# Two-layer gated cross-attention with routed experts on one core: layer 0 written as one block; in layer 1 the last head group ahead of the end of the ranking, its transfers on two queues, the biases loaded last

## The chip, the core and the metric

The program runs on one core of a Trainium2 chip. A core has five engines that run their own instruction streams and meet only at semaphores: TensorE (PE, matrix products into the PSUM banks; PEld are its weight loads), VectorE (DVE), ScalarE (ACT), GpSimd (POOL) and SyncE (SP, which mostly issues transfers). Transfers run on 16 DMA engines that all queues share. The metric is the device time of one execution in microseconds, lower is better.

## What is computed

A sequence `x` of 2048 rows of 256 values passes through two layers. Each layer adds gated cross-attention to a context of 1601 rows of 192 values (16 heads of 16), then a gated expert network:

```python
x = x + tanh(g_xattn[0]) * cross_attention_0(layernorm(x), ctx)      # softmax over 1601 keys, then Wo
x = x + tanh(g_ffn[0])   * (shared_swiglu(h) + top1_expert_swiglu(h * sigmoid(max_logit)))   # h = layernorm(x)
x = x + tanh(g_xattn[1]) * mlp(cross_attention_1(layernorm(x), ctx)) # relu(o @ W1 + b1) @ W2 + b2
h = layernorm(x)
y = mixed_top2_experts(h) + h          # relu(h @ W1[e] + b1[e]) @ W2[e] + b2[e], weighted by a softmax of two logits
x = x + tanh(g_ffn[1]) * (gamma * layernorm(y) + beta)
```

There are 8 experts in each layer.

## The kernel before

The 2048 rows stand on 128 partitions, 16 tiles of 128 rows. Every engine has its own program, written out in the order in which it runs; a wait on a semaphore holds up all that is behind it on that engine. A *block* is a piece of program for all five engines: at its end the engines meet in a barrier before the next one starts.

Layer 0 is made of three blocks. The first is the **preparation** (`prepare(0)`): it loads `x`, the context and weights, normalizes, projects keys, queries and values, writes bf16 parts of them to DRAM, and ends with `unsafe`, a flag that says whether the scores could overflow. The second block opens with `asked`: each engine loads `unsafe` into a register and branches, and normally jumps over a part that finds the largest scores. Then comes **attention**: four query blocks of 512, four groups of four heads each, 13 chunks of 128 keys in each (52 steps `w` for each query block). `scores` (L1539) makes the scores, ACT the exponentials (L1868), `weigh` (L1564) the weighted values. For each group DVE copies the result, spreads the sum of the exponentials, takes the reciprocal and multiplies (`group_copy`, `group_norm`, and `last_group` for the very last group, which does it in two halves), and SP moves four heads of it to where the projection reads them (L2487, and `gather_last`, L2497, with eight transfers for the halves). After attention come the shared experts, the routing, and the keys of layer 1. The third block is the **expert loop**: POOL fetches the rows of a tile by index (`fetch_rows`, L1145), PE turns them (`turn_rows`, L1242), DVE or ACT copies them, `up` (L1255) and `down` (L1269) are the two products, and POOL stores the result by index (L1456). This block goes on with the preparation of layer 1 and ends in a barrier that also clears the semaphores.

Layer 1 is one more block. Its last part matters here. Twelve of its sixteen row tiles are ranked early: in step `COUNTS_AT` = 44 of the last query block `counts_first` counts them on PE, then `rank_first` on DVE works out each token's slot, builds one-hot rows (`in_row`, L2282, for 24 slots in one instruction) and the expert of each tile; `lists_first` on PE (L1710) turns them into lists, and `places` on DVE into row numbers, on which POOL's fetches and ACT's copies of expert weights wait. Behind `rank_first` DVE adds the bias of the projection to `x` and runs `own_tail`: `last_group`, `places`, then the work on the projection. PE runs `lists_first`, then `keep_warm` (products of the identity with itself into a bank nobody reads, L466), then `last_projection` (L1786, L1795), whose halves wait for the two halves of the last head group, then the expert loop. In this loop ACT works on the 17 early tiles (`first_scalar`) and POOL adds the bias `eb2`; DVE meanwhile ranks the rest. SP loads the down weights of the 8 experts (L1199, 512 KB each) and their biases spread over the partitions (L1195, 128 KB each) in turn, then `gamma` and `beta`. `down(0)` waits for all sixteen loads:

```python
if i == 0:
    pe.wait_ge(s_e, 16 * (2 if l else 3) * E)
```

## Time and profile before

| | us |
|---|---|
| median of 3 runs | 1403.71 |
| lowest, highest run | 1403.46, 1404.62 |
| the profiled execution | 1401.74 |
| its span, first to last instruction | 1400.0 |
| mean granted PE clock in it | 0.985 of full |
| PE, ACT, DVE, POOL busy | 1324.1, 987.5, 721.0, 193.8 |

Times in rows are counted from the start of the span. The profiled execution is 1.74 us longer than its span and 1.97 us shorter than the median of the runs. The clock of PE is either full (2.4 GHz) or half of it (1.2 GHz), so a value between means a stretch with both. A row of the timeline gives start, duration, engine, line, operation and shapes, and in brackets how long the engine had been idle and what it had waited for. Products of f32 values take two passes and so count as two instructions: the 12 of `keep_warm` show as x24.

### The profile page before, as it was taken

How to read it: one execution, taken by the hardware profiler on the slowest of the kernel's cores; microseconds unless marked ns; L12 is line 12 of the kernel's file. 1: busy time of each engine (PE TensorE's matmuls, PEld its weight loads, DVE VectorE, ACT ScalarE, POOL GpSimd, SP SyncE). 2: the span in 40 equal slices, each digit the busy share in tenths (PEclk: the TensorE clock that was granted, in tenths of full speed). 3: DMA queues.
4: the chain of work that ended last, by engine and by line, in shares of the span. 5: the costliest groups of instructions: out<-in, count | busy, mean ns of one | idle time of the engine just before them, and what ended most of it. 6: DMA issues, size and time to landing. Idle time of an engine off the chain costs nothing. (4 is left out here: it accounts for less than half of the span.)

```text
span 1400.0 us, 33588 instructions
## 1 busy us (share of the span) xinstructions
PE 1324.1 (95%) x13844; PEld 729.6 (52%) x13844; DVE 721.0 (52%) x1415; ACT 987.5 (71%) x1263; POOL 193.8 (14%) x211
## 2 busy tenths in 40 slices
PE   7899999999999999899988999999999997999994
PEld 4433343343433555899964333433433533889983
DVE  7466634544352435433356474585485487442436
ACT  4699999999999334223256998798799695376532
POOL 2000000000000232133220000000000000287740
PEclk9999999999999999999998999999999999999998
DMA  7771010010110642411147500020010130522214
GB/s 204 184 131 29 21 28 18 21 30 21 30 27 20 228 156 71 136 50 50 35 123 187 104 21 18 17 59 21 17 59 21 51 111 25 191 65 70 76 60 175
DMA packets 66966, 103.53 MB, mean 74 GB/s; under 512 B 10524, under 2 KB 48674, under 8 KB 65916
## 3 DMA queue, kind: packets, MB, share of 16 engines
q1 hardware_dynamic: 60860, 85.10, 22.2%
q0 software_dynamic: 5952, 16.26, 3.7%
q8 instruction: 111, 1.82, 0.6%
q14 instruction: 43, 0.35, 0.1%
HBM read 69.04 MB, written 27.79 MB: 69 GB/s over the span
## 5 line engine op out<-in xcount | busy, mean ns | idle before, releaser
L1868 ACT ACTIVATE arena<-ps 128x1024 f32<-128x1024 f32 x528 | 521.1, 1151 | 47.1 <-PE ps L1539 46.1
L1539 PE MATMUL ps<-arena 99*32 99x512 bf16 x6528 | 454.0, 385 | 11.3 <-issue 7.6
L1539 PEld LDWEIGHTS ps<-arena 99*32 99x32 bf16 x6528 | 167.6, 96 | 372.1 <-issue 163.0
L1564 PE MATMUL ps<-arena 128*32 128x512 f32 x2176 | 333.8, 596 | 0.6 <-ACT xn L1861 0.4
L1868 ACT ACTIVATE wqkv<-ps 128x1024 f32<-128x1024 f32 x260 | 269.3, 1144 | 21.2 <-PE ps L1539 21.1
L1564 PE MATMUL ps<-wqkv,arena 128*32 128x512 f32 x1056 | 186.4, 593 | 0.1
L1255 PE MATMUL ps<-work,arena 128*128 128x128 f32 x1184 | 144.5, 277 | 2.0 <-DVE work L1344 1.0
L1255 PEld LDWEIGHTS ps<-work,arena 128*128 128x128 f32 x1184 | 142.9, 194 | 5.7 <-DVE work L1344 1.5
L1269 PE MATMUL ps<-arena,work 128*128 x496 | 117.6, 380 | 2.0 <-DMA arena<-in_eb 1.6
L1564 PEld LDWEIGHTS ps<-arena 128*32 128x32 f32 x2176 | 79.7, 111 | 58.2 <-issue 4.7
L2019 DVE RECIPROCAL work<-work 128x512 f32<-128x512 f32 x30 | 100.6, 3353 | 1.0
L1269 PEld LDWEIGHTS ps<-arena,work 128*128 128x128 f32 x496 | 89.4, 190 | 12.7 <-issue 3.0
L1145 POOL DMA_INDIRECT work<-xn_early,fetch x17 | 21.1, 1243 | 491.8 <-DVE fetch L2372 474.6
L2592 POOL TENSOR_TENSOR arena<-arena 128x512 f32<-128x512 f32 x12 | 17.5, 1458 | 477.7 <-ACT arena L1888 477.7
L1316 ACT ACTIVATE work<-ps 128x512 f32<-128x512 f32 x23 | 13.8, 598 | 98.0 <-PE ps L1255 98.0
L1154 ACT ACTIVATE arena<-arena 128x1024 f32 x62 | 65.5, 1059 | 18.8 <-DVE fetch L2372 12.1
L1456 POOL DMA_INDIRECT y_tok<-work,dest x62 | 62.1, 1002 | 117.0 <-DVE work L1370 83.5
L1344 DVE COPY work<-ps 128x256 f32<-128x256 f32 x45 | 19.1, 424 | 97.7 <-PE ps L1242 82.7
L2010 DVE SCALAR_TENSOR_TENSOR work<-xn,last_v,ps 128x512 f32<-128x512 f32 x30 | 22.4, 745 | 81.6 <-PE ps L1564 81.3
L2105 DVE TENSOR_TENSOR work<-ps,b 128x512 f32<-128x512 f32 x14 | 9.7, 691 | 94.0 <-PE ps L1597 94.0
L1564 PEld LDWEIGHTS ps<-wqkv,arena 128*32 128x32 f32 x1056 | 43.7, 111 | 25.5 <-issue 0.6
L1973 DVE TENSOR_SCALAR xn<-ps 128x1024 f32<-128x1024 f32 x12 | 14.7, 1224 | 78.5 <-PE ps L1539 78.5
(327 smaller groups left out, 1477.7 us busy)
## 6 DMA issues: line engine op xcount, KB each, us to landing
arena<-in_ew SPq DMA_DIRECT2D x16, 512.0 KB, 4.7
arena<-q_img SPq DMA_DIRECT2D x32, 192.0 KB
arena<-y_tok SPq DMA_DIRECT2D x12, 512.0 KB, 7.0
arena<-k_img SPq DMA_DIRECT2D x8, 624.0 KB, 12.9
q_img<-work SPq DMA_DIRECT2D x18, 256.0 KB, 2.8
k_img<-work SPq DMA_DIRECT2D x21, 208.0 KB, 2.5
arena<-q_img SPq DMA_DIRECT2D x32, 128.0 KB
arena<-in_rg SPq DMA_DIRECT2D x8, 512.0 KB, 7.1
```

Source lines behind the costliest of these rows:

```text
L1145: nc.gpsimd.indirect_dma_start(out=rows_in[i % ROWBUFS], out_offset=None, in_=xn_early if i < L.first else xn_img[l], in_offset=bass.Indir ...
L1154: nc.scalar.activation(w_now[i % 2][0].rearrange("p k n -> p (k n)"), w_gate[l][:, bass.ds(e, 1), :, :].rearrange("p a k n -> p (a k n)"), ...
L1255: last = nc.tensor.matmul(ps[:, 2 + 2 * (i % 2) + n, f * P:(f + 1) * P], w_now[i % 2][n][:, k, f * P:(f + 1) * P], rowsT[i % 2][:, k, :], ...
L1269: last = nc.tensor.matmul(ps[:, 6 + i % 2, 0:D], hT[i % 2][:, k, :], w_down[:, bass.ds(e, 1), k, :].rearrange("p a n -> p (a n)"), start=( ...
L1344: nc.vector.tensor_copy(rowsT[i % 2], ps[:, i % 2, 0:D].rearrange("p (k n) -> p k n", n=P)).then_inc(s_tc, 1)
L1456: nc.gpsimd.indirect_dma_start(out=y_tok[l], out_offset=bass.IndirectOffsetOnAxis(ap=dest[:, i:i + 1], axis=0), in_=rows_out[i % 2], in_of ...
L1539: last = nc.tensor.matmul(ps[i * VW:(i + 1) * VW, buf + j, :], keys, q2[0:ROWS + SHIFT, h, :], start=True, stop=True, skip_group_check=True)
L1564: last = nc.tensor.matmul(ps[j * VW:(j + 1) * VW, 6 + g % 2, :], v_aug[:, c, HG * g + j, :], exps, start=(c == 0), stop=(c == NC - 1), ski ...
L1868: nc.scalar.activation(probs[n % RING], ps[:, buf:buf + 2, :], ACT.Exp, scale=SCALE).then_inc(s_exp, 1)
L2010: nc.vector.scalar_tensor_tensor(out=pv_sb, in0=last_exp[:, g % 2, :], scalar=last_v[:, g:g + 1], in1=ps[:, 6 + g % 2, :], op0=ALU.mult, o ...
L2019: nc.vector.reciprocal(sums, sums).then_inc(s_inv, 1)
L2592: nc.gpsimd.tensor_tensor(sh_hT[:, f, :], sh_hT[:, f, :], sh_act[:, n % 2, :], ALU.mult).then_inc(s_hm, 1)
```

## The change

**Layer 0 in one block.** The three blocks become one. Each engine runs its preparation, its attention part and its expert loop without a barrier between them. What the barriers ensured is now waited for: `asked` waits for a semaphore on `unsafe`, PE for the copied values and POOL's padding of them ahead of its part, SP for the sums of key norms ahead of `loop_sync`.

**Layer 1.** `COUNTS_AT` goes from 44 to 42. `rank_first` stops after half of the one-hot rows; then comes `last_group`, then the second half, the expert numbers and the rest as before. `keep_warm` is called with 24 ahead of `lists_first` and with 4 behind it, instead of with 12 behind it. `gather_last` runs on SP for heads 0 and 1 and on ACT, ahead of `first_scalar`, for heads 2 and 3. SP loads the eight down weights first and then the eight biases, which count on `s_ln` now; `down(0)` waits for the weights alone, POOL and DVE for `s_ln`.

In `group_norm` and `last_group` two semaphores of their own become the chain that the rest of DVE's program uses, with the same waits.

```diff
-COUNTS_AT = 44
+COUNTS_AT = 42
@@ pad_v
-                chain(nc.gpsimd.memset(v_aug[other, NC - 1, i::2, 0:DH], 0.0))
+                last = nc.gpsimd.memset(v_aug[other, NC - 1, i::2, 0:DH], 0.0)
+            last.then_inc(s_vpad, 1)
@@ prepare, tensor
-                if l == 1:
+                if l == 0:
+                    pe.wait_ge(s_va, NC)
+                    pe.wait_ge(s_vpad, 1)
+                else:
                     keep_warm(3, 8)
@@ prepare, vector
-                chain(nc.vector.tensor_scalar(unsafe[0:1, :], tops[0:1, 2:3], SAFE * SAFE / SCALE ** 2, None, ALU.is_gt))
+                nc.vector.tensor_scalar(unsafe[0:1, :], tops[0:1, 2:3], SAFE * SAFE / SCALE ** 2, None, ALU.is_gt).then_inc(s_un, 1)
@@ layer
-            if l == 0:
-                with nc.Block() as block:
...
-                    block.gpsimd(prep_pool)
...
             def asked(eng):
+                eng.wait_ge(s_un, l + 1)
                 return eng.If(eng.value_load(unsafe[0:1, 0:1], min_val=0, max_val=1) > 0)
@@ load_biases
-                eng.dma_start(eb2[:, e, :], spread(a["eb2"][e], D)).then_inc(s_e, 16)
+                eng.dma_start(eb2[:, e, :], spread(a["eb2"][e], D)).then_inc(s_ln, 16)
...
+            def gather_last(eng, heads):
+                g = NG - 1
+                for i in range(2):
+                    cols = slice(i * 2 * P, (i + 1) * 2 * P)
+                    eng.wait_ge(s_on, NB * NG + i)
+                    for j in heads:
+                        h = HG * g + j
+                        eng.dma_start(oT[(h % 8) * DH:(h % 8 + 1) * DH, h // 8, cols],
+                                      o_norm[j * VW:j * VW + DH, g % 2, cols]
+                                      ).then_inc(s_oh2 if i else s_oc[g % 2], 16)
@@ loop_tensor, down
-                        pe.wait_ge(s_e, 16 * (2 if l else 3) * E)
+                        pe.wait_ge(s_e, 16 * (1 if l else 3) * E)
@@ loop_vector, and loop_pool likewise
-                    dve.wait_ge(s_ln, 32)
-                    dve.wait_ge(s_e, 16 * 2 * E)
+                    dve.wait_ge(s_ln, 16 * (2 + E))
@@
             def first_scalar(act, between):
+                gather_last(act, range(HG - 2, HG))
                 act.wait_ge(s_pl, 1)
@@ tensor
+                    if l == 0:
+                        prep_tensor(pe)
                     max_tensor(pe)
@@ lists_first
-                        pe.wait_ge(s_row, 1)
                         for i in range(of.slots):
+                            if i % (of.slots // 2) == 0:
+                                pe.wait_ge(s_row, i // (of.slots // 2) + 1)
@@
                     if l == 1:
+                        keep_warm(0, 24)
                         lists_first()
-                        keep_warm(0, 12)
+                        keep_warm(0, 4)
                         last_projection()
...
                         k_norm(3)
+                        loop_tensor(pe)
@@ vector, own_tail
-                        last_group()
                         places(first_lists, 6, 0)
@@ rank_first
-                        lists_of(of, end, L.pieces()[0], 0, 1)
+                        lists_of(of, L.pieces()[0])
+                        rows_of_lists(of, 0, 2)
+                        return end
@@
-                        rank_first()
+                        end = rank_first()
+                        last_group()
+                        rows_of_lists(first_lists, 1, 2)
+                        experts_of_lists(first_lists, end, 0)
@@ sync
-                    gather_last()
+                    gather_last(sp, range(HG - 2 * l))
                     sp.wait_ge(s_pv, NB * NG * NC)
...
                             load_down(sp, e)
+                        for e in range(E):
                             load_biases(sp, e)
...
-                    if l == 1:
-                        loop_sync(sp)
+                    if l == 0:
+                        sp.wait_ge(s_kn, 4)
+                    loop_sync(sp)
@@ end of layer
-            if l == 0:
-                with nc.Block() as block:
-                    block.sync(loop_sync)
...
-                    block.gpsimd(loop_pool)
```

The instructions of PE between the end of attention in layer 1 and the expert loop, before (L1564 are the last weighings, L1710 the lists, L466 the warming products, L1786 and L1795 the projection):

```order
L1564 MATMUL ps<-wqkv,arena 32x512 x2
L1564 MATMUL ps<-arena 32x512 x10
L1710 MATMUL ps<-ctxT 128x36 x24
L466 MATMUL ps<-ident 128x128 x12
L1786 MATMUL ps<-work,w 128x256 x16
L1795 MATMUL ps<-w,work 128x256 x16
```

and after:

```order
L1568 MATMUL ps<-wqkv,arena 32x512 x2
L1568 MATMUL ps<-arena 32x512 x10
L466 MATMUL ps<-ident 128x128 x24
L1717 MATMUL ps<-ctxT 128x36 x24
L466 MATMUL ps<-ident 128x128 x4
L1793 MATMUL ps<-work,w 128x256 x16
L1802 MATMUL ps<-w,work 128x256 x16
```

Twice as many warming products stand ahead of the lists, and the lists' second half has a wait of its own inside its row.

DVE in the same place, before (L2282 the one-hot rows, L2042 to L2054 the last head group, L2360 the first operation of the places):

```order
L2282 TENSOR_TENSOR ctxT<-iota_row,rankf 128x3072
L2287 TENSOR_TENSOR ctxT<-iota_tile,ends 128x119
L2290 TENSOR_REDUCE tilef<-ctxT 128x17
L2291 CAST tile_e<-tilef 128x17
L2406 SCALAR_TENSOR_TENSOR x<-b,tgate,x 128x512 x2
L2042 SCALAR_TENSOR_TENSOR work<-xn,last_v,ps 128x512
L2046 STREAM_SHUFFLE work<-work 128x512
L2050 RECIPROCAL work<-work 128x256
L2054 TENSOR_TENSOR work<-work 128x256
L2050 RECIPROCAL work<-work 128x256
L2054 TENSOR_TENSOR work<-work 128x256
L2360 COPY pad<-ps 128x17
```

and after:

```order
L2290 TENSOR_TENSOR ctxT<-iota_row,rankf 128x1536
L2052 SCALAR_TENSOR_TENSOR work<-xn,last_v,ps 128x512
L2056 STREAM_SHUFFLE work<-work 128x512
L2059 RECIPROCAL work<-work 128x256
L2062 TENSOR_TENSOR work<-work 128x256
L2059 RECIPROCAL work<-work 128x256
L2062 TENSOR_TENSOR work<-work 128x256
L2290 TENSOR_TENSOR ctxT<-iota_row,rankf 128x1536
L2297 TENSOR_TENSOR ctxT<-iota_tile,ends 128x119
L2300 TENSOR_REDUCE tilef<-ctxT 128x17
L2301 CAST tile_e<-tilef 128x17
L2426 SCALAR_TENSOR_TENSOR x<-b,tgate,x 128x512 x2
```

The head group stands ahead of the second half of the one-hot rows, of the expert numbers and of the bias, with the places behind all of them.

## Rows read from the trace of the kernel before

**Rows 1.** Part 1 of the page: busy time, share, instructions.

```profile
PE 1324.1 (95%) x13844; PEld 729.6 (52%) x13844; DVE 721.0 (52%) x1415; ACT 987.5 (71%) x1263; POOL 193.8 (14%) x211
```

**Rows 2.** Timeline, preparation to attention in layer 0: start, us, engine, line, operation.

```profile
59.74 0.60 PE L906 MATMUL ps<-ident,top 128*1 128x128 f32 x4
...
61.00 0.14 DVE L979 TENSOR_SCALAR unsafe<-tops 1x1 int32<-1x1 f32 x1
61.19 0.27 SPq L525 DMA_DIRECT2D last_value<-work  x1
63.30 6.91 PE L1539 MATMUL ps<-arena 99*32 99x512 bf16 x60 [2.96 <-issue]
```

**Rows 3.** Timeline, shared experts to expert loop in layer 0.

```profile
567.40 0.51 PE L472 MATMUL ps<-head_rows,w 128*104 128x16 bf16 x8
...
567.63 2.02 SPq L1199 DMA_DIRECT2D arena<-in_rd  x4
...
568.98 0.42 DVE L2472 TENSOR_REDUCE norms<-ps 104x4 f32<-104x256 f32 x1
...
570.31 0.41 PE L1242 MATMUL ps<-ident,work 128*128 128x128 f32 x2 [2.40 <-PEq L1510]
...
570.76 0.42 DVE L1344 COPY work<-ps 128x256 f32<-128x256 f32 x1 [1.37 <-PE ps L1242]
...
571.24 5.47 PE L1255 MATMUL ps<-work,arena 128*128 128x128 f32 x32 [0.52 <-DVE work L1344]
```

**Rows 4.** Stretches: us, busy (count) per engine, then PE clock, DMA share, GB/s.

```profile
63.30:73.25 9.95, 9.91 (x84) 3.02 (x88) 5.23 (x9) 6.77 (x8) 0.00 (x0) 0.50 0.85 170
571.60:575.10 3.50, 3.50 (x20) 3.50 (x19) 0.86 (x1) 0.00 (x0) 0.34 (x1) 0.51 1.04 340
745.80:749.20 3.40, 1.81 (x16) 1.34 (x14) 2.54 (x7) 0.00 (x0) 0.00 (x0) 1.00 0.83 280
1185.50:1189.50 4.00, 4.00 (x10) 3.19 (x11) 0.69 (x2) 2.00 (x2) 2.91 (x3) 0.50 0.46 119
```

**Rows 5.** Timeline, end of attention and start of the projection in layer 1.

```profile
1160.86 0.36 DVE L2254 COPY ctxT<-ps 128x192 f32<-128x192 f32 x1 [2.20 <-PE ps L1649]
...
1172.06 3.35 DVE L2282 TENSOR_TENSOR ctxT<-iota_row,rankf 128x3072 bf16<-128x3072 f32 x1
...
1174.00 1.06 PE L1564 MATMUL ps<-arena 128*32 128x512 f32 x8 [0.21 <-ACT xn L1861]
...
1176.16 2.92 PE L466 MATMUL ps<-ident 128*128 128x128 f32 x24
1177.51 0.75 DVE L2042 SCALAR_TENSOR_TENSOR work<-xn,last_v,ps 128x512 f32<-128x512 f32 x1
...
1181.77 4.93 SPq L2497 DMA_DIRECT2D work<-work  x8
1183.39 0.42 DVE L2054 TENSOR_TENSOR work<-work 128x256 f32<-128x256 f32 x1
...
1185.50 9.11 PE L1786 MATMUL ps<-work,w 128*128 128x256 f32 x32 [6.41 <-DMA work<-work]
...
1187.58 0.48 DVE L2067 TENSOR_SCALAR work<-ps,b 128x256 f32<-128x256 f32 x1 [2.17 <-issue]
```

**Rows 6.** Stretch under the loads, then timeline of the expert loop in layer 1.

```profile
1195.00:1207.00 12.00, 10.16 (x59) 8.59 (x58) 6.27 (x25) 1.51 (x5) 0.95 (x1) 1.00 1.08 344
...
1209.85 1.99 PE L1269 MATMUL ps<-arena,work 128*128 x8 [1.55 <-DMA arena<-in_eb]
...
1240.67 5.71 POOL L1145 DMA_INDIRECT work<-xn_early,fetch  x1 [0.30 <-issue]
1240.70 4.62 DVE L2282 TENSOR_TENSOR arena<-iota_row,rankf 128x1024 bf16<-128x1024 f32 x4
...
1248.22 0.44 PE L1242 MATMUL ps<-ident,work 128*128 128x128 f32 x2 [1.64 <-DMA work<-xn_early,fetch]
...
1248.74 0.97 POOL L1145 DMA_INDIRECT work<-xn_early,fetch  x1 [0.31 <-PE ps L1242]
```

More of the change, by code:

```diff
@@ L996, in layer @@
              stored, load_q2) = preps[l]
-            if l == 0:
-                with nc.Block() as block:
-                    @block.sync
-                    def _(sp):
-                        prep_loads(sp)
-                        prep_sync(sp)
-                    block.scalar(prep_scalar)
-                    block.tensor(prep_tensor)
-                    block.vector(prep_vector)
-                    block.gpsimd(prep_pool)
             s_hq, s_ms, s_mm, s_mt, s_mc, s_mo, s_md = (
@@ L2016, in group_norm @@
                         dve.wait_ge(s_u, n)
[L2017 to L2020 removed]
+                        chain(nc.vector.stream_shuffle(out=sums, in_=pv_sb, mask=[DH] * VW))
+                        chain(nc.vector.reciprocal(sums, sums))
                         if g >= 2 or not (b == 0):
@@ L2261, in scan_of, with lists_of @@
                         return of.scan[i], of.scan[1 - i]
-                    def lists_of(of, end, pieces, at, row_pieces):
+                    def lists_of(of, pieces):
                         n, w = of.slots, of.cols
@@ L2278, in lists_of, with rows_of_lists, experts_of_lists @@
                         last.then_inc(s_tok, 1)
-                        for i in range(row_pieces):
-                            m = n // row_pieces
-                            js = slice(i * m, (i + 1) * m)
-                            nc.vector.tensor_tensor(of.in_row[:, js, :],
-                                                    iota_row[:, :].unsqueeze(1).broadcast_to([P, m, P]),
-                                                    rankf[:, js].unsqueeze(2).broadcast_to([P, m, P]), ALU.is_equal
-                                                    ).then_inc(s_row, 1)
+                    def rows_of_lists(of, i, row_pieces):
+                        m = of.slots // row_pieces
+                        js = slice(i * m, (i + 1) * m)
+                        nc.vector.tensor_tensor(of.in_row[:, js, :],
+                                                iota_row[:, :].unsqueeze(1).broadcast_to([P, m, P]),
+                                                rankf[:, js].unsqueeze(2).broadcast_to([P, m, P]), ALU.is_equal
+                                                ).then_inc(s_row, 1)
+                    def experts_of_lists(of, end, at):
                         m = of.tiles
@@ L2352, in rank_rest @@
                                                              in1=rankf[:, 0:n], op0=ALU.add, op1=ALU.mult))
-                        lists_of(of, end, L.pieces()[1], L.first, PIECES)
+                        lists_of(of, L.pieces()[1])
+                        for i in range(PIECES):
+                            rows_of_lists(of, i, PIECES)
+                        experts_of_lists(of, end, L.first)
                     def places(of=None, bank=6, at=0):
@@ L2488, in gather_heads @@
                                          o_norm[j * VW:j * VW + DH, g % 2, :]).then_inc(s_oc[g % 2], 16)
-                    def gather_last():
-                        g = NG - 1
-                        for i in range(2):
-                            cols = slice(i * 2 * P, (i + 1) * 2 * P)
-                            sp.wait_ge(s_on, NB * NG + i)
-                            for j in range(HG):
-                                h = HG * g + j
-                                sp.dma_start(oT[(h % 8) * DH:(h % 8 + 1) * DH, h // 8, cols],
-                                             o_norm[j * VW:j * VW + DH, g % 2, cols]
-                                             ).then_inc(s_oh2 if i else s_oc[g % 2], 16)
                     def over_group(g):
```

38 lines of the change are left out of this document (20 added, 18 removed).

## The prediction

> **What bounds the kernel now.** I read the page first: TensorE (PE) is busy for 95% of the span [rows 1], so most of the time can't be moved by a change of waits. What can be moved are the holes in PE's row and the stretches in which its granted clock is 0.50 of full (1.2 of 2.4 GHz). Next I read the timeline around each place that the diff touches, and the clock of those stretches. There are four: the boundary between the preparation of layer 0 and its attention [rows 2], the boundary between its shared experts and its expert loop [rows 3], the hand-over from attention to the projection in layer 1 [rows 5], and the first down projection of the expert loop in layer 1 [rows 6]. At all four PE stands still, and nothing else in the kernel is moved by the edits except later by the same amount, because behind each of them PE goes on with work that follows it one after another.
>
> **Boundary one.** Before, PE ends its two transposing products at 60.34 us, VectorE (DVE) writes `unsafe` from 61.00 to 61.14, the sync engine (SP) issues its last store until 61.46, and the first score starts at 63.30 [rows 2]. Two things lie in the 1.84 us from 61.46: leaving and entering a block, and the load of `unsafe` with its branch. The second boundary holds the block change alone: SP's last issue ends at 567.63 + 2.02 = 569.65, PE starts at 570.31, so 0.66 us [rows 3]. That leaves 1.84 - 0.66 = 1.18 us for load and branch, which stay. In the new code they start when `unsafe` is there: 61.14 + 1.18 = 62.32 instead of 63.30, a gain of 0.98 us. The bounds are 0.3 (if the branch also waits for instructions that the block change used to hide) and 1.5 us (if load and branch take no longer than a block change, 0.66). ScalarE starts right behind the scores in both, so the gain isn't given back there. The clock is 0.50 from 63.30 to 73.25 [rows 4] and I leave that as it is.
>
> **Boundary two.** PE ends at 567.91. DVE ends its last reduction at 568.98 + 0.42 = 569.40. Everything then waits for SP, whose four loads of down weights wait for the last shared product and take until 569.65. Turned rows come at 570.31, DVE copies them at 570.76, PE's first expert products start at 571.24 [rows 3]. In the new code PE turns the rows at once, at 567.9; the copy stands on DVE behind the reduction and starts at about 569.45, so the products start 570.76 - 569.45 = 1.3 us earlier. SP's loads are on nobody's path: the down weights are needed ten us later. Then there is the clock. PE was busy for only 0.41 us between 567.91 and 571.24, and from 571.6 to 575.1 the clock was 0.51 [rows 4], with PE busy all of those 3.50 us: half of them, 1.7 us, are lost. The new gap is 1.6 us long: from the end of the turned rows at 567.9 + 0.4 to the products at 571.24 - 1.3 = 569.9. The nearest stretch with so much idle time is 745.80 to 749.20, busy 1.81 of 3.40 us, and there the clock stayed 1.00 [rows 4]. I take the gain of 1.7 us as the likelier case; the bounds are 0 and 1.7.
>
> **The hand-over in layer 1, start.** Before, DVE waited 2.20 us for the counts until 1160.86. Two steps earlier (each step is some 1.7 us of PE) they are there before DVE is free, so the ranking starts 2.2 us earlier. The one-hot rows took 3.35 us from 1172.06; the first half of them is now done by 1172.06 - 2.2 + 1.7 = 1171.6. PE's last weighing ends at 1175.06. The last head group, which started at 1177.51 behind the ranking, starts at about 1175.1, 2.4 us earlier. It took until 1183.39 + 0.42 = 1183.81, 6.30 us, so it now ends at 1181.4 [rows 5]. Behind it DVE makes the second half of the one-hot rows, 1.7 us, until 1183.1. PE needs that for the lists: they took 0.75 us (1175.41 to 1176.16), half of it is 0.4, and four of the warming products of 2.92 / 12 = 0.24 us follow, 1.0 us. PE starts the projection at 1183.1 + 0.4 + 1.0 = 1184.5, against 1185.50: a gain of 1.0 us. The transfers don't decide that. Before, eight took 4.93 us to issue, 0.62 each, the first 4.26 us behind the start of the group, and PE started 1185.50 - (1181.77 + 3 x 0.62) = 1.9 us after the issue of the fourth began. With two per queue the first half lands by 1175.1 + 4.3 + 0.6 + 1.9 = 1181.9, and the second half, ready at 1181.4, by 1183.9. ScalarE has nothing to do from 1175 on, so its waits for the group hold up nobody. A transfer issued on ScalarE isn't in the trace; it may cost nothing beyond SP's 0.62, or as much as the 0.97 us that GpSimd (POOL) takes at 1248.74 [rows 6]; two such would still leave the first half in before 1184.5, so I take the cost as 0. The bounds of this gain: it is 3.6 us if the lists don't hold PE back (a start at 1181.9), and 0 if DVE's small gaps add up. What stands behind the second half on DVE is 2.10 us of small work (1175.41 to 1177.51) and the places, 1.60 us (1187.58 - 2.17 - 1183.81): they end at 1183.1 + 2.1 + 1.6 = 1186.8. The first hidden values follow at 1186.8 instead of 1187.58 [rows 5], and PE asks for the first of them 3.5 us after 1184.5. They are not late; POOL's fetches and ScalarE's weight copies start 1.4 us later than before, with over ten us to spare.
>
> **The hand-over, clock.** Before, PE had nothing from 1179.08 to 1185.50 and ran at 0.50 until 1189.50, 4.0 us of products [rows 4, 5]: 2.0 us lost. Now 24 warming products stand ahead of the lists and last 24 x 0.24 = 5.8 us, from 1175.1 to 1180.9, the first half of the lists goes to 1181.3, and the gap to 1183.1 is 1.8 us. That again is like 745.80 to 749.20, which didn't fall. I count 2.0 us; bounds 0 and 2.0.
>
> **Biases last.** The first down projection waited 1.55 us for the last bias transfer, at 1209.85 [rows 6]. It now waits only for the weights: 8 x 512 KB = 4.2 MB, which at 344 GB/s [rows 6] take 12.2 us. SP issues four transfers less and gets to them at some 1182.7, so they are in by about 1196, ten us before they are needed. The biases follow in 3 us and are first read by POOL behind that product. The gain is 1.55 us, with no bound below 1.5 that I can find.
>
> **The sum**, against the profiled execution: 0.98 + 1.3 + 1.7 + 1.0 + 2.0 + 1.55 = 8.5 us. Its span of 1400.0 us becomes 1391.5, its time of 1401.74 us becomes 1393.2. The median of the runs is 1403.71, 1.97 above that; the change does nothing to what makes this difference, so the forecast for the median is **1395.2 us**.
>
> **Rivals.** (a) The clock falls at one of the two shortened gaps all the same. For it: at 571.6 it fell after 3.3 us with little work, not after a long pause, and where the fall comes is not in the kernel's hands. Against it: the row at 745.80. Price 1.7 or 2.0 us, so 1397.1; both, 1398.9. (b) The clock doesn't fall at boundary one either, since that gap shrinks from 3.0 to 2.0 us. PE at 0.50 made ScalarE wait: it was busy 6.77 of 9.95 us [rows 4]. At most 2 us more: 1393.2. (c) The stalled fetch. POOL's fetch at 1240.67 took 5.71 us beside DVE's 4.62 us of one-hot rows, against 0.97 us for the next one, and PE waited 1.64 us for it [rows 6]. If that is one engine keeping the other out and the two meet otherwise now, up to 1.6 us more are gained: 1393.6. Both hang on ScalarE's pace in the loop, which doesn't change, so I expect the same meeting. The Trainium skill (SBUF — State Buffer, Who interferes with whom) says that a `tensor_tensor` of DVE has no mode that takes the write port which GpSimd needs to write descriptors, and that only its reads contend. By that rule the 5.71 us would be no lock, and its place would be open; the trace shows the length of the four DVE instructions in it, and speaks against the rule. (d) The slower side: the second half of the group, now on two queues, comes in behind the weights. SP goes on to 4.2 MB of loads as soon as its own two transfers are issued, 4 us earlier than before, and does not wait for ScalarE's two. If these were served only behind all 5.3 MB (15.4 us at 344 GB/s [rows 6], until 1198), PE would stand 10 us at 1188 and start cold, 2.0 us: 1395.2 + 10 + 2 = 1407.2. It decides once they land after 1188; they are issued by 1183, and five us are over. (e) The blocks bring nothing, because the same waits show up behind them: without 0.98 and 1.3 and the clock of boundary two, 1399.2.
>
> **How the numbers follow.** Forecast as summed 0.42, (a) 0.28, (b) 0.12, (c) 0.05, (e) 0.08, (d) 0.03, something unseen 0.02. The range from 1392.0 to 1399.8 holds (b) and (c) together at its lower end and (e) at its upper end, with (a). 0.2% is 2.8 us, about what a measurement can tell from no change here; faster by more means below 1400.9, which all cases but (d) and a sum of several misses reach: faster 0.91, within 0.2% 0.06, slower 0.03.
>
> **What would show it.** In the new profile: the first score at about 62.3; PE's first expert product some 1.3 us behind where shared work ends plus DVE's reduction, and a clock of 1.00 behind it; the last group's copy right behind the last weighing; PE's gap before the projection below 2 us and the projection in 7 us instead of 9.11; no wait before the first down projection. It is wrong if the lists or DVE's places, not PE's own work, set the end of the projection, if the clock falls at both gaps, or if a row transfer lands late under the loads.

## The result and the profile after

The changed kernel took 1395.78 us (median of five runs, 1392.27 to 1396.55) against 1403.46 us (five runs, 1401.84 to 1404.62): a ratio of 0.994, interval 0.9928 to 0.9953. With 1395.2 forecast, the time fell where it was expected. The profiled execution took 1396.19 us, its span is 1394.4 us: 5.6 us less than the 1400.0 us of before, not 8.5. That gap is what most of the experiments are about.

First a row each of the page's parts 1 and 2, to be read beside [rows 1]:

```profile
PE 1324.3 (95%) x13876; PEld 734.4 (53%) x13876; DVE 721.2 (52%) x1416; ACT 985.6 (71%) x1263; POOL 192.9 (14%) x211
...
PEclk9999999999999999999999999999999999999997
```

Boundary one, the timeline of the changed kernel (beside [rows 2]):

```profile
59.77 0.60 PE L907 MATMUL ps<-ident,top 128*1 128x128 f32 x4
...
61.04 0.14 DVE L983 TENSOR_SCALAR unsafe<-tops 1x1 int32<-1x1 f32 x1
61.22 0.26 SPq L525 DMA_DIRECT2D last_value<-work  x1
62.60 4.25 PE L1543 MATMUL ps<-arena 99*32 99x512 bf16 x44 [2.23 <-issue]
```

From the end of `unsafe` to the first score it is now 1.42 us; it was 63.30 - 61.14 = 2.16.

Boundary two (beside [rows 3]):

```profile
564.06 0.51 PE L472 MATMUL ps<-head_rows,w 128*104 128x16 bf16 x8
...
564.29 2.02 SPq L1192 DMA_DIRECT2D arena<-in_rd  x4
564.43 0.41 PE L1246 MATMUL ps<-ident,work 128*128 128x128 f32 x2
...
565.64 0.42 DVE L2492 TENSOR_REDUCE norms<-ps 104x4 f32<-104x256 f32 x1
565.97 0.41 DVE L1348 COPY work<-ps 128x256 f32<-128x256 f32 x1
...
566.44 3.84 PE L1259 MATMUL ps<-work,arena 128*128 128x128 f32 x32 [1.60 <-DVE work L1348]
```

TensorE (PE) turns the rows under SP's four loads (row SPq L1192), and the first expert product starts 2.38 us behind the start of the last norm products, not 3.84. The hand-over in layer 1 (beside [rows 5]):

```profile
1154.16 0.36 DVE L2261 COPY ctxT<-ps 128x192 f32<-128x192 f32 x1
...
1170.47 5.62 PE L466 MATMUL ps<-ident 128*128 128x128 f32 x48
1170.61 0.75 DVE L2052 SCALAR_TENSOR_TENSOR work<-xn,last_v,ps 128x512 f32<-128x512 f32 x1 [3.50 <-PE ps L1568]
...
1174.41 3.53 ACTq L1203 DMA_DIRECT2D work<-work  x4
1174.45 3.22 SPq L1203 DMA_DIRECT2D work<-work  x4
...
1176.59 1.76 DVE L2290 TENSOR_TENSOR ctxT<-iota_row,rankf 128x1536 bf16<-128x1536 f32 x1
...
1178.41 0.47 PE L1717 MATMUL ps<-ctxT 128*128 128x36 bf16 x12 [2.01 <-DVE ctxT L2290]
...
1180.06 8.38 PE L1793 MATMUL ps<-work,w 128*128 128x256 f32 x32
```

The last group follows the last weighing at once, and the second half of the lists holds PE back, as the prediction had it. The ranking ahead of them starts 16.4 us before the last weighing ends (DVE takes the counts at 1154.16 us, without a wait), against 14.2 us before. The projection took 8.38 us, though, not 7. The clock (last figure but two) of six stretches says why:

```profile
63.10:66.50 3.40, 3.40 (x40) 1.19 (x32) 0.00 (x0) 3.23 (x4) 0.00 (x0) 0.51 0.87 183
66.50:70.00 3.50, 2.98 (x48) 0.95 (x44) 3.22 (x5) 3.02 (x5) 0.00 (x0) 0.99 1.03 156
566.50:570.00 3.50, 3.50 (x31) 3.50 (x32) 0.55 (x1) 0.00 (x0) 0.04 (x1) 1.00 1.04 351
718.50:725.30 6.80, 5.63 (x13) 3.45 (x14) 4.14 (x27) 2.23 (x4) 0.00 (x0) 0.50 0.01 2
...
1176.00:1179.40 3.40, 1.39 (x30) 1.29 (x29) 3.20 (x7) 0.00 (x0) 0.00 (x0) 0.98 0.15 35
1179.40:1182.80 3.40, 3.40 (x12) 2.86 (x11) 2.68 (x10) 0.00 (x0) 0.38 (x1) 0.51 0.98 330
```

No fall behind boundary two (566.50), as hoped. At the hand-over the clock fell at 1179.3, for 3.4 us. At boundary one it is low for 3.4 us and not for ten. And between 718.5 and 725.3 there is a fall that the first trace of before doesn't have. This is where the lead went: the changed kernel was 6.4 us ahead at 708 us and only 0.9 us at the first score of layer 1 (752.27 against 753.21).

The way there begins with VectorE (DVE), which adds the returned expert rows of layer 0 to x. In the changed kernel:

```profile
702.66 1.28 DVE L1410 SCALAR_TENSOR_TENSOR x<-arena,tgate,x 128x1024 f32<-128x1024 f32 x1 [7.96 <-DMA arena<-y_tok]
...
707.07 1.28 DVE L1410 SCALAR_TENSOR_TENSOR x<-arena,tgate,x 128x1024 f32<-128x1024 f32 x1 [3.12 <-DMA arena<-y_tok]
```

The second transfer landed 3.1 us late. The normalized rows of layer 1 came that much later, PE stood twice for 1.9 us, and its clock fell. Is that the change's doing, or chance?

### The profile page after: what moved, and what is told of

Its sections match the earlier page's. It is cut to its first block and busy times, and to the rows that moved or that the text cites. A ratio compares the mean times of both kernels' runs of the same rounds, so it can differ in the third digit from the quotient of the medians.

```text
span 1394.4 us, 33627 instructions
## 1 busy us (share of the span) xinstructions
PE 1324.3 (95%) x13876; PEld 734.4 (53%) x13876; DVE 721.2 (52%) x1416; ACT 985.6 (71%) x1263; POOL 192.9 (14%) x211
## 5 line engine op out<-in xcount | busy, mean ns | idle before, releaser
L1459 POOL DMA_INDIRECT y_tok<-work,dest x62 | 61.6, 993 | 116.4 <-DVE work L1374 83.0
```

Source lines behind the costliest of these rows:

```text
L1459: nc.gpsimd.indirect_dma_start(out=y_tok[l], out_offset=bass.IndirectOffsetOnAxis(ap=dest[:, i:i + 1], axis=0), in_=rows_out[i % 2], in_of ...
```

## The experiments

Each variant is the changed kernel with the edit shown, unless said otherwise. Single executions spread over more than ten us (the kernel before: 1398.4 to 1409.9 in 22 runs), so the medians settle only the larger effects, and the smaller ones are read in the traces. This table gives, for every trace, the time between two rows, in us: **a** end of `unsafe` to first score of layer 0; **b** that score to the end of the last weighing of layer 0; **c** start of the last norm products to first expert product; **d** from there to the value projection behind the loop; **e** first identity product of layer 1's preparation (row PE L466, x60) to its first score; **f** end of the last weighing of layer 1 to the second half of the projection (row PE L1802 of the changed kernel); **g** from there to the first down projection; **h** from there to the second lists.

```
                     a      b      c      d      e      f      g      h
before             2.16 395.38   3.84 129.26  38.89  19.38  15.41  48.60
before, again      2.29 395.24   3.83 127.64  44.23  18.95  15.93  50.49
changed            1.42 392.75   2.38 127.63  44.38  17.74  13.70  49.10
changed, again     1.43 392.66   2.37 127.63  39.38  16.07  13.69  49.84
first boundary     2.14 392.93   2.38 128.25  42.30  17.75  13.69  49.86
second boundary    1.43 392.91   3.84 129.19  42.01  17.71  13.69  49.11
biases between     1.42 393.08   2.38 127.63  38.82  17.73  13.70  49.82
one queue, biases  1.43 394.45   2.37 127.96  44.64  16.07  16.93  50.20
lists later        1.43 392.99   2.37 127.64  39.45  14.08  13.69  50.31
rows apart         1.42 395.49   2.37 128.77  39.69  16.06  13.70  46.19
rows at once       1.43 394.45   2.37 127.63  42.25  16.06  13.69  45.90
four warming       1.42 392.38   2.37 128.45  40.19  17.62  13.69  48.84
together           1.43 392.67   2.37 127.80  38.13  14.09  13.69  45.89
warming between    1.42 393.10   2.38 127.63  42.17  16.05  13.69  49.25
```

**The changed kernel again.** No edit.

> The changed kernel once more, for a second trace and more times. In its first trace VectorE waited 3.12 us at 707.07 for the second of the four transfers that bring layer 0's expert rows back, and a lead of 6.4 us over the kernel before (570 us) had shrunk to 0.9 us at 752 us. Theory: that transfer is late by chance in some executions, so this trace may show no such wait (lead of 5 us or more at 752 us, span of 1389 to 1391 us) and the times spread over 1391 to 1397 us with a median near 1395. Rival: the change itself makes it late (layer 0's loop now starts 6.4 us earlier in the work of another queue), and then the wait of about 3 us is there again and the span is near 1394.

It took 1393.23 us (eight runs, 1388.81 to 1400.33), ratio 0.9932 (0.9905 to 0.996); its profiled span is 1387.0 us. DVE waited 0.90 us for the second transfer, e is 39.38 us, and the first score of layer 1 came 5.9 us ahead of before's. So column e is chance by up to 5 us. Whether the change adds to it was asked of the kernel before.

**The kernel before again.** No edit.

> The kernel before once more, for a second trace. In eight of nine traces of the changed kernel and its variants VectorE waits 0.9 to 3.1 us for the second transfer that brings layer 0's expert rows back; in the one trace of the kernel before it didn't. Theory: the arrival is chance, and this trace shows such a wait too (0.9 us or more near 710 us); the stretches at half clock (10.2, 3.4, 10.2 and 6.8 us in the first trace) come at other places or with other lengths. Rival: the kernel before is free of that wait, and the change pays for its earlier start with it: no wait again, and the same four stretches.

```profile
708.36 1.28 DVE L1407 SCALAR_TENSOR_TENSOR x<-arena,tgate,x 128x1024 f32<-128x1024 f32 x1 [7.98 <-DMA arena<-y_tok]
712.77 1.29 DVE L1407 SCALAR_TENSOR_TENSOR x<-arena,tgate,x 128x1024 f32<-128x1024 f32 x1 [3.13 <-DMA arena<-y_tok]
```

The kernel before waits 3.13 us here as well, and then its e is 44.23 us and its clock is low from 723.9 to 730.7. The late landing doesn't need the change: the first trace of before was an execution without it, and that cost 5.5 us (e: 44.38 against 38.89) in the comparison of two single executions. Whether the change makes it commoner isn't shown: DVE waited 0.7 to 3.6 us there in eleven of the twelve traces of the changed kernel and its variants, and in one of the two of before. The clock's stretches moved too: here it did not fall behind boundary two (d is 127.64, as in the changed kernel), where the prediction had taken the fall as a property of the code.

**First boundary back.**

```diff
+            if l == 0:
+                with nc.Block() as block:
...
+                    block.scalar(prep_scalar)
+                    block.tensor(prep_tensor)
...
                     if l == 0:
-                        prep_tensor(pe)
```

> The changed kernel with the block change between layer 0's preparation and its attention put back. Theory: the first score starts 0.7 us later than in the changed kernel (63.3 instead of 62.6 us), and in addition TensorE stays at half clock until about 73 us instead of 66.6 us, which makes another 2.6 us: 3.3 us slower than the changed kernel, median near 1399. Rival: the length of that stretch is chance and has nothing to do with the boundary: 0.7 us slower, median near 1396.5.

Median 1394.32 us, ratio 0.9935 (0.9911 to 0.9958). Column a is 2.14 us again, 0.72 more. Column b is 392.93 us: the clock was low for 3.4 us only, with the boundary in place. The theory that the block change makes the long stretch falls in this form; 0.7 us is what the boundary costs, and the median, 0.4 us under the 1394.7 us of the changed kernel's thirteen runs, doesn't resolve that. The last section comes back to the length of the stretch.

**Second boundary back.**

```diff
                         k_norm(3)
-                        loop_tensor(pe)
...
+            if l == 0:
+                with nc.Block() as block:
+                    block.sync(loop_sync)
+                    block.tensor(loop_tensor)
```

> The changed kernel with the block change between layer 0's shared experts and its expert loop put back. Theory: the first expert product comes 1.5 us later again (3.8 instead of 2.4 us behind the last k norm), and the clock falls to half for 3.4 us behind it, 1.6 us more: 3.1 us slower than the changed kernel, median near 1398.9. Rival (the blocks bring nothing, the same waits come back further on): no difference, median near 1395.8; if only the start is lost and the clock stays, 1397.3.

```profile
564.00 0.51 PE L472 MATMUL ps<-head_rows,w 128*104 128x16 bf16 x8
...
566.92 0.41 PE L1246 MATMUL ps<-ident,work 128*128 128x128 f32 x2 [2.40 <-PEq L1514]
...
567.84 5.39 PE L1259 MATMUL ps<-work,arena 128*128 128x128 f32 x32 [0.52 <-DVE work L1348]
```

Median 1397.58 us (twelve runs), ratio 0.9959 (0.994 to 0.9977), 2.9 us over the changed kernel's 1394.7. Column c is 3.84 us, 1.47 more, and the 32 products take 5.39 instead of 3.84 us at half clock. The rival (the blocks bring nothing) is out. With the block change the clock fell here in two of three traces; without it in none of the other eleven.

**Biases between the weights again.**

```diff
                         for e in range(E):
                             load_down(sp, e)
-                        for e in range(E):
                             load_biases(sp, e)
...
-                        pe.wait_ge(s_e, 16 * (1 if l else 3) * E)
+                        pe.wait_ge(s_e, 16 * (2 if l else 3) * E)
```

> The changed kernel with the eight bias transfers of layer 1 issued between the down weights again and waited for by the first down projection. Theory: that product waits 1.6 us again, less what the transfers now start earlier (6 to 9 us before their old time): the loads start 9 us earlier than before against a loop that starts 6 us earlier, so the wait may shrink to nothing in this kernel. I expect 0.0 to 0.5 us of it, median near 1396. Rival: the last bias transfer comes 1.5 us or more behind its need as before, and the median is near 1397.5.

Median 1395.08 us, ratio 0.9936 (0.9912 to 0.9959). Column g stays at 13.70 us: no wait. In this execution the order of the biases, to which the prediction gave 1.55 us, is worth nothing. SP begins these loads at 1173.00 us and the product starts 24.3 us later; in the kernel before they began at 1186.74 and the product started 23.1 us later [rows 6], after a wait. But part of the 24.3 us is the clock: it fell at the projection here (f is 17.73) and put the product 1.7 us later. In the changed kernel's second trace it didn't fall:

```profile
1172.72 7.99 SPq L1192 DMA_DIRECT2D arena<-in_ew  x8
...
1195.30 1.89 PE L1273 MATMUL ps<-arena,work 128*128 x8
```

There the product starts 22.6 us behind the first load. Loads that take 23.1 us with the biases between would be 0.5 us late in such an execution; that is an estimate from these rows, and no run shows it.

**One queue, and the biases between the weights.** The same with

```diff
-                gather_last(act, range(HG - 2, HG))
...
-                    gather_last(sp, range(HG - 2 * l))
+                    gather_last(sp, range(HG))
```

> The changed kernel with two of its parts undone together: all eight row transfers of the last head group on the sync engine's queue, and the bias transfers between the down weights again. With the biases alone put back, the first down projection of layer 1 didn't wait (the loads began 23.9 us ahead of it there, 21.6 us in the kernel before, which waited 1.55 us). Theory: the wait went because SP gets to its loads earlier, and the order of biases is worth nothing by itself. Here four more issues hold the loads back by 1.7 us or so: they begin about 22.3 us ahead of the product, so a wait of 0.3 to 1.0 us comes back. The projection starts as in the changed kernel (9.4 us behind the last weighing), because the lists hold it, not the transfers. Rival: one queue alone holds the projection back as well, by 1 us or more; or no wait at all is seen, and then the loads have more slack than the first trace showed.

```profile
1205.06 1.99 PE L1273 MATMUL ps<-arena,work 128*128 x8 [3.07 <-DMA arena<-in_eb]
```

Median 1395.87 us, ratio 0.9951 (0.9931 to 0.997). The wait is back, 3.07 us, more than expected: SP begins the loads 21.0 us ahead of the need, and they take 24.1. The lead is 3.3 us shorter than in the variant above. Half of that are the eight issues on SP's queue (4.93 us instead of 3.22), the other half is the clock, which didn't fall at the projection here (f is 16.07 instead of 17.73). So the second queue does bring something, not to the projection (which starts 9.16 us behind the last weighing, to the hundredth what the changed kernel's second trace shows), but to the loads behind it on SP: 1.7 us. That it alone removes the wait is seen once, in an execution with the fall. The order of the biases alone, on one queue, was not run; the 1 MB of biases takes 3.0 us at the 344 GB/s of [rows 6] (an estimate), about what the product waits here.

**Warming products between the halves of the lists.**

```diff
                             if i % (of.slots // 2) == 0:
+                                if i:
+                                    keep_warm(0, 7)
                                 pe.wait_ge(s_row, i // (of.slots // 2) + 1)
```

> The changed kernel with seven more warming products (0.24 us each, 1.7 us) between the two halves of the lists in layer 1, in the 2.0 us in which TensorE waits for VectorE's second half of the one-hot rows. Theory: in four of the five traces with the new hand-over (the changed kernel's first one and three variants) the clock fell to half for 3.4 us within 1 us of the projection's start, because TensorE had too little work around that gap; with the gap filled it stays at full, the projection's first 32 products take 7.0 instead of 8.4 us, and the projection doesn't start later. 1.4 us faster than the changed kernel in such executions, median 1.0 us lower (its own, over 13 times, is 1394.7). Rival: the fall is not tied to that gap, and comes all the same: no difference. Slower side: if the seven products outlast the wait, the projection starts up to 0.3 us later.

Median 1395.34 us (ten runs), ratio 0.993 (0.9907 to 0.9953). In its trace the clock stayed and the projection took 7.07 us (f = 16.05). But the changed kernel's own second trace has 16.07 without the edit. Over the nine traces with the changed order of this hand-over (the one-queue variant among them) the clock fell at the projection in five, f = 17.6 to 17.8, and not in four, f = 16.06 or 16.07. One trace without a fall proves nothing, and the median shows no gain: inconclusive.

**Second half of the lists later.**

```diff
                                 last.then_inc(s_full7, 1)
+                                if half == 0 and f == 1:
+                                    lists_first(1)
...
                         for half in range(2):
+                            if half:
+                                places(first_lists, 6, 0)
```

> The changed kernel with the second half of the lists put behind the first two output tiles of the projection instead of ahead of it, and the places behind the first four outputs on VectorE. Theory: the lists hold the projection back in the changed kernel (TensorE waited 2.0 us for the one-hot rows while the transfers were in); it then starts when the first half of the last head group has landed, 1.5 to 2.0 us earlier than in the changed kernel (7.4 to 7.9 us behind the last weighing instead of 9.4), and the clock doesn't fall near it: 3 us in all, median near 1391.7. Rival one: the transfers end as late as the lists (first half in at about 9 us behind the last weighing), gain 0.3 us or less. Rival two: VectorE's places, now in the middle, hold the second half of the projection back, and what is won at its start is lost at its end: near 1394.7.

```profile
1172.79 0.46 PE L1717 MATMUL ps<-ctxT 128*128 128x36 bf16 x12
1173.09 1.14 PE L466 MATMUL ps<-ident 128*128 128x128 f32 x8
1174.07 1.95 PE L1794 MATMUL ps<-work,w 128*128 128x256 f32 x8
1175.85 0.46 PE L1717 MATMUL ps<-ctxT 128*128 128x36 bf16 x12
```

Median 1391.26 us, ratio 0.9912 (0.9889 to 0.9935). One of its six runs took 2794.62 us, twice the others, for no reason that the record shows; the median of the other five is 1390.65. The projection starts 6.7 us behind the last weighing instead of 9.2, right behind the warming products, so the rows were in; f is 14.08, 2.0 less than the best of the changed kernel. This shows what the prediction only argued: the lists held PE back, not the transfers.

**Rows of the second lists apart.**

```diff
                         for i in range(PIECES):
+                            dve.wait_ge(s_y, 8 + i)
                             rows_of_lists(of, i, PIECES)
```

> The changed kernel with the four pieces of one-hot rows of the second lists (1.15 us each) no longer one behind the other on VectorE: each waits until the next tile's result is copied out (one per 3.73 us). In all six traces so far GpSimd's fetch that starts together with these pieces takes 5.72 us instead of 0.96, and TensorE then waits 1.3 to 1.6 us for it. Theory: VectorE's pieces keep GpSimd from writing the fetch's descriptors as long as they run back to back; apart, each meets GpSimd while it adds or waits, no fetch takes over 2.2 us, TensorE doesn't wait, and the clock can't fall behind that wait: 2 us faster than the changed kernel, median near 1392.5. Rival: the length of that fetch has another cause (its rows, a full queue); it is 5.7 us again at the same tile, and nothing is gained.

First the fetch of the changed kernel, then of the variant:

```profile
1232.38 5.72 POOL L1138 DMA_INDIRECT work<-xn_early,fetch  x1 [0.30 <-issue]
1232.42 4.61 DVE L2290 TENSOR_TENSOR arena<-iota_row,rankf 128x1024 bf16<-128x1024 f32 x4
...
1239.93 0.44 PE L1246 MATMUL ps<-ident,work 128*128 128x128 f32 x2 [1.31 <-DMA work<-xn_early,fetch]
```

```profile
1229.16 1.23 DVE L2290 TENSOR_TENSOR arena<-iota_row,rankf 128x1024 bf16<-128x1024 f32 x1 [1.08 <-issue]
1229.31 1.65 POOL L1453 TENSOR_TENSOR work<-work,arena 128x256 f32<-128x256 f32 x1 [0.39 <-DMA y_tok<-work,dest]
...
1232.56 0.96 POOL L1138 DMA_INDIRECT work<-xn_early,fetch  x1 [0.30 <-issue]
1232.88 1.23 DVE L2290 TENSOR_TENSOR arena<-iota_row,rankf 128x1024 bf16<-128x1024 f32 x1 [2.49 <-ACT work L1498]
```

Median 1392.03 us, ratio 0.9919 (0.9902 to 0.9936). No fetch is long, PE doesn't wait for one between 1220 and 1345 us, and h is 46.19 instead of 48.8 to 50.3 us. In five of the eleven traces with a long fetch the clock also fell for 3.4 us behind PE's wait for it (h 49.8 to 50.5). GpSimd (POOL) pays at its additions, 1.65 instead of 0.73 us, which nobody waits for.

**The same rows at once, behind one wait.**

```diff
+                        dve.wait_ge(s_y, 8)
                         for i in range(PIECES):
                             rows_of_lists(of, i, PIECES)
```

> The changed kernel with the four pieces of one-hot rows back to back again, but the first of them held back until the next tile's result is copied out, as in the variant with the pieces apart. There the pieces met GpSimd's additions, and the fetch took 0.96 us. Theory: pieces that run back to back keep out whichever descriptors GpSimd writes meanwhile; now it is the store of the expert rows, issued about 1 us behind the first piece, that is stretched from 1.0 to 3.5 us or more (until the fourth piece ends), and TensorE waits 1 us or more for the fetch behind it, or for the additions. Rival: only that one fetch is slow by nature; then the store takes 1.0 us, and the fetch of that tile 5.7 us again or not at all.

```profile
1234.99 5.16 DVE L2290 TENSOR_TENSOR arena<-iota_row,rankf 128x1024 bf16<-128x1024 f32 x4 [1.08 <-issue]
1235.15 1.66 POOL L1453 TENSOR_TENSOR work<-work,arena 128x256 f32<-128x256 f32 x1 [0.38 <-DMA y_tok<-work,dest]
...
1237.09 1.69 POOL L1459 DMA_INDIRECT y_tok<-work,dest  x1 [0.28 <-POOL work L1453]
...
1239.08 1.92 POOL L1138 DMA_INDIRECT work<-xn_early,fetch  x1 [0.30 <-issue]
```

One execution, 1393.08 us. Neither theory holds. The store lies wholly within the four pieces and took 1.69 us, not 3.5; the fetch took 1.92, and h is 45.90 us, the gain in full. In the eleven traces in which the pieces meet a fetch it takes 5.24 to 5.72 us; it starts between 0.04 us ahead of and 0.45 us behind the first piece and always ends 1.06 or 1.07 us behind the last, as if it had been let in only then. Here the pieces (5.16 us in all instead of 4.61, of which the second took 1.75) begin beside POOL's addition, and a store that starts among them gets through. What makes the one run of pieces a lock and the other not stays open; it was not tried further.

**Four warming products at the end of layer 1's preparation.**

```diff
-                    keep_warm(3, 8)
+                    keep_warm(3, 4)
```

> The changed kernel with 4 instead of 8 warming products at the end of layer 1's preparation. In the changed kernel's trace the decision value of layer 1 is ready at 748.37 us, the eight products last until 749.54, and the first score starts 2.73 us behind these; in the kernel before it also starts 2.73 us behind them. Theory: the products outlast what the block change needs to wait for, so four fewer (0.96 us) let the first score start 1.0 us earlier (2.7 us behind the decision value instead of 3.9). 1 us faster, unless the clock's stretch at half gets longer. Rival: the block change waits for something else (a store of the sync engine), and the first score stays 3.9 us behind the decision value.

Median 1395.54 us, ratio 0.9928 (0.9905 to 0.9951). From the end of `unsafe` to the first score it is 2.97 us; it is 3.9 in every trace with eight. The 0.9 us are there; the median doesn't resolve them.

**Three together.** Lists later, rows apart, four warming products.

> The changed kernel with three of the variants together: the second half of the lists inside the projection, the four pieces of one-hot rows apart, four warming products instead of eight at the end of layer 1's preparation. By the traces of the three alone: projection 2.0 us shorter from the last weighing to its second half and no fall of the clock there (1.7 us in most executions), 2.4 to 2.9 us at the fetch, 0.9 us at the first score of layer 1. Theory: they add up, 5 to 7 us faster than the changed kernel (1394.7), median near 1389. Rival: the fetch's place and the earlier projection meet otherwise (with the lists later alone, TensorE waited 2.1 us for that fetch instead of 1.3), and no more than 4 us are left: 1391.

1387.87 us (five runs, 1382.16 to 1389.48), ratio 0.9898 (0.988 to 0.9916): 14 us under the kernel before and 7 us under the changed one, the upper end of what was expected, and the only variant whose interval lies below that of the changed kernel's first set (0.9928 to 0.9953). f is 14.09 and h 45.89, as with each edit alone: they add up.

## Why the prediction was right, and where it wasn't

The time was right and the starts were each right to 0.3 us; the terms for the clock were not, and part of the agreement is luck with it. Measured from the table:

- **Boundary one, 0.98 forecast:** 0.73 (a: 2.2 to 1.42). The split of 1.84 us into 0.66 for the block and 1.18 for load and branch was off: load and branch take 1.42 behind `unsafe`.
- **Its clock, left as it was:** wrong in the favourable way. b was 395.2 and 395.4 in the two traces of before and 393.1 or less in eight of the eleven traces without the boundary (394.5 in two, 395.5 in one), 2.0 us less on average. That is rival (b)'s mechanism in another shape: the clock still fell, for a shorter time, and only one of the eleven had no fall (b is 392.38). The short stretch gave 2.4 us where it happened. It isn't shown to be the change's doing: it came with the boundary put back as well, and in layer 1 untouched by any edit.
- **Boundary two, 1.3 and 1.7:** 1.47, and 1.6 when the clock falls in the kernel before. It did so in two of three traces with the block change, so the term is worth about 1.1 on three traces.
- **The hand-over, 1.0 and 2.0:** together 1.5 with a fall at the projection (five traces of nine), 3.1 without (f against the mean of before's two, 19.2). The mechanism (ranking earlier, lists as the last thing waited for) was right to 0.3 us at the projection's start. That the lists are last is tested by an edit; the earlier counts, DVE's new order and the 24 warming products were not undone one by one, and their share is read from the trace. The step that failed is the likeness to the stretch at 745.80 [rows 4]: PE was busy for 1.39 us of 3.40, not 1.81. Nor does that figure decide alone. The second trace of the changed kernel has the same 1.39 us and kept its clock:

```profile
1170.70:1174.10 3.40, 1.39 (x31) 1.28 (x30) 3.20 (x7) 0.00 (x0) 0.00 (x0) 1.00 0.19 42
1174.10:1177.50 3.40, 3.40 (x20) 3.07 (x20) 2.94 (x11) 0.00 (x0) 0.08 (x1) 1.00 0.95 305
```

- **Biases last, 1.55:** g fell by 1.7 to 2.2 us, but no run shows that the order did it. Weights and biases together, put at 15.4 us in rival (d) by the 344 GB/s of [rows 6], took 23.1 us from SP's first issue before and 24.1 with one queue. They were needed 21.6 us behind that issue before, 24.3 in the changed kernel with a fall at the projection and 22.6 without. "With no bound below 1.5" was the overconfident step: the prediction noted that SP gets to the loads earlier, and didn't ask whether that alone was enough. It is where the clock falls, and by estimate 0.5 us short where it doesn't.
- **"Nothing else is moved except later by the same amount"** was the claim that single executions broke. Column e is 41.6 us on average in the two traces of before and 41.5 in the ten with the same warming products, so it holds as far as these few tell; in one trace the return of the expert rows moved the lead by 5.5 us.
- **Rival (a)** came true at the projection in five traces of nine and never at boundary two. **(c)** didn't come: the fetch was 5.7 us again beside the same rows, and its gain had to be fetched by an edit. **(d)** found no support: no wait of PE for a row transfer in any trace with the change. **(e)** fell with the second boundary put back. The range's ends were loosely worked out: (b) and (c) together give 1395.2 - 2 - 1.6 = 1391.6, and (e) with a fall at the projection 1401.2, both outside 1392.0 to 1399.8.

The sum of what the table shows is 0.73 + 1.47 + 1.1 + 2.2 (1.5 and 3.1, five to four) + 2.0 = 7.5 us. The medians differ by 7.7 us in the first set and, by the ratio of 0.9932, by 9.5 in the second. The rest, up to 2 us, fits column b, which the sum leaves out: 2.0 us on average. So the agreement with 8.5 us has luck in it: the shorter stretches at the start of attention made up for the falls at the projection.

## What to carry to other kernels

When one profiled execution loses what the medians show, take a second trace of both kernels before explaining anything: a late transfer and a moved clock stretch shifted single spans of this kernel by five us. Credit an edit with the removal of a wait only after putting that edit alone back, because a neighbour that makes a queue free earlier can pay for the same wait, and so can a fall of the clock ahead of it. And where two engines meet for long, move one of them by a wait that costs nothing: here a single wait on VectorE ended a fetch of 5.7 us and took 2.6 to 4.4 us off the stretch around it.

## What the runs showed of the chip

The stretch of half clock at the start of attention has three lengths, and its length goes with when the clock fell, counted from PE's first score. In 14 traces there are 28 such starts. In eight the clock fell 0.2 us or more ahead of the first score, and it stayed low for 10.2 us each time. In sixteen it fell within 0.1 us of the score or behind it: for 3.4 us in the thirteen in which it came up to 0.7 us behind, for 6.8 us in the three in which it came 0.9 to 1.1 us behind. In four there was no fall. The first kind in the variant with rows apart, where the clock fell at 61.6 us and the score started at 61.98:

```profile
61.80:65.20 3.40, 3.22 (x32) 1.31 (x36) 0.00 (x0) 2.12 (x3) 0.00 (x0) 0.50 0.44 110
65.20:68.60 3.40, 3.37 (x32) 0.76 (x28) 1.99 (x3) 2.85 (x4) 0.00 (x0) 0.50 1.08 206
68.60:72.00 3.40, 3.40 (x32) 1.03 (x28) 3.31 (x6) 1.86 (x3) 0.00 (x0) 0.53 0.97 184
```

Beside it stands the row at 63.10 of the changed kernel above: score at 62.60, fall at about 63.1, PE busy for 3.40 of 3.40 us, and the clock was back at 66.6. In column b the long kind costs 2.1 to 2.8 us more than the short one. With the first boundary in place two of three starts of layer 0 were of the long kind, without it one of eleven; no run moved the fall by itself, so this is a reading of coincidences and not a tested cause.

The Trainium skill (SBUF — State Buffer, Who interferes with whom) says that a `tensor_tensor` of VectorE doesn't take the write port that GpSimd's descriptors need. The prediction held the trace against that. The same section says that such an instruction with both inputs in SBUF does contend with what GpSimd reads there. The Trainium skill (SBUF — State Buffer, Summary: rules for kernel authors) adds that the second of the two to issue is then blocked until the first has finished. The one-hot rows have both inputs in SBUF, and the fetch has its row numbers there, so the long fetch may be a matter of reads, and the prediction read the rule too narrowly. The traces agree as far as the fetch of 5.24 to 5.72 us goes. They don't in three things: in six of the eleven the fetch began 0.03 to 0.04 us ahead of the first piece and was held all the same (POOL's spans are rough), four separate instructions act as one lock, and a store among the same instructions took 1.69 us.
